# A five-layer graph network on one core: the second edge layer of the gathered group moved to the head of TensorE's step

## The reference

```python
def _leaky(x):
    return jax.nn.leaky_relu(x, negative_slope=0.1)
for l in range(W1.shape[0]):
    h = _leaky(x @ W1[l] + b1[l]) @ W2[l] + b2[l]
    e = _leaky(edge_attr @ We1[l] + be1[l]) @ We2[l] + be2[l]
    msg = h[src] * e * dot_scale[l]
    agg = jax.ops.segment_sum(msg, dst, num_segments=n)
    out = x + agg * res_w[l]
    mu = jnp.mean(out, axis=-1, keepdims=True)
    var = jnp.mean(jnp.square(out - mu), axis=-1, keepdims=True)
    x = (out - mu) * jax.lax.rsqrt(var + LN_EPS) * ln_g[l] + ln_b[l]
```

## Time and profile before

| | |
|---|---|
| median of 3 runs | 6457.28 us (6454.09 to 6462.97) |
| profiled execution | 6457.48 us, of which the trace's span is 6455.7 us |
| PE, matmuls | 5500.8 us busy, 85% of the span |
| DVE | 5171.0 us, 80% |
| POOL | 4527.6 us, 70% |
| ACT | 1134.5 us, 18% |
| mean granted clock of TensorE | 0.889 of 2.4 GHz |

### The profile page before, as it was taken

One profiled execution on the slowest core, in us unless ns is written; L12 is line 12 of the kernel. 1 busy time (PEld: TensorE's weight loads), 2 busy tenths in 40 slices (PEclk: granted clock), 3 DMA queues, 4 the chain that ended last, 5 costly groups with the idle time before them and its releaser, 6 DMA issues.

```text
span 6455.7 us, 169151 instructions
## 1 busy us (share of the span) xinstructions
PE 5500.8 (85%) x63332; PEld 3612.2 (56%) x63333; DVE 5171.0 (80%) x7991; ACT 1134.5 (18%) x1726; POOL 4527.6 (70%) x4793
## 2 busy tenths in 40 slices
PE   6776899998889788989878898888898887888887
PEld 2222444456666555666645666655566664556665
DVE  8997644598888688988859888867898885998886
ACT  0000311111222211122211122221112221111111
POOL 5777777766777367777737777756777773777775
PEclk9998555699999889999979999988999996999997
DMA  3112299855666455666635566644566663666664
GB/s 138 26 24 46 61 244 243 196 140 141 147 147 164 106 126 133 153 148 159 162 82 137 146 150 150 165 119 116 134 152 148 154 168 77 143 148 159 160 171 110
DMA packets 733545, 886.20 MB, mean 137 GB/s; under 512 B 325488, under 2 KB 502976, under 8 KB 731568
## 3 DMA queue, kind: packets, MB, share of 16 engines
q1 hardware_dynamic: 568480, 703.64, 42.4%
q0 software_dynamic: 152144, 154.93, 12.1%
q10 hardware_dynamic: 12096, 16.53, 0.8%
HBM read 749.51 MB, written 125.06 MB: 135 GB/s over the span
## 4 chain that ended last, share of the span: by engine, by line
PE 50%; DVE 18%; issue 14%; POOL 12%; DVEq 3%; ACT 2%; DMA 1%; ACTq 0%; SPq 0%; POOLq 0%
PE bank L981 12%; POOL arena L794 12%; PE bank L1030 8%; PE bank L1054 5%; PE bank L977 5%; PE bank L923 4%; PE bank L880 3%; PE bank L1017 3%; PE bank L861 2%; DVE arena L1765 2%; PE bank L846 2%; DVE arena L1423 2%; DVE arena L1677 2%; PE bank L902 2%; DVE arena L1432 2%
## 5 line engine op out<-in xcount | busy, mean ns | idle before, releaser
L794 POOL DMA_INDIRECT arena<-h_rows,src x3855 | 3674.2, 953 | 1555.7 <-issue 1246.5
L981 PEld LDWEIGHTS bank<-w2s,arena 128*128 128x128 f32 x8960 | 1143.7, 206 | 928.9 <-DVE arena L1765 694.9
L981 PE MATMUL bank<-w2s,arena 128*128 128x128 f32 x8960 | 1271.3, 298 | 412.5 <-DVE arena L1765 363.5
L781 POOL DMA_INDIRECT slots<-arena,slot_index x792 | 787.7, 995 | 267.2 <-issue 241.3
L1054 PEld LDWEIGHTS bank<-arena 112*64 112x64 f32 x20160 | 647.5, 139 | 287.9 <-issue 269.5
L1054 PE MATMUL bank<-arena 112*64 112x64 f32 x20160 | 733.2, 226 | 58.9 <-issue 53.8
L977 PE MATMUL bank<-x_packed,edge_w 64*128 64x512 f32 x1260 | 713.5, 647 | 0.8 <-DMA x_packed<-slot_attr 0.7
L1253 ACT ACTIVATE arena<-bank,tenth 128x512 f32<-128x512 f32 x490 | 335.6, 685 | 2125.1 <-PE bank L977 2125.1
L977 PE MATMUL bank<-nodes_state,edge_w 64*128 64x512 f32 x980 | 568.6, 661 | 105.5 <-DVE nodes_state L1746 66.6
L1685 DVE TENSOR_TENSOR x_packed<-bank,slot_rel 128x2880 f32<-128x2880 f32 (+8 forms) x315 | 592.4, 1881 | 49.3 <-issue 42.7
L1685 DVE TENSOR_TENSOR arena<-bank,slot_rel 128x2880 f32<-128x2880 f32 (+8 forms) x315 | 592.3, 1880 | 45.8 <-issue 39.3
(11 more groups left out here) (198 smaller groups left out, 5682.2 us busy)
## 6 DMA issues: line engine op xcount, KB each, us to landing
arena<-slot_pick SPq DMA_DIRECT2D x630, 448.0 KB
arena<-h_rows SPq DMA_DIRECT2D x630, 224.0 KB
x_packed<-slot_attr SPq DMA_DIRECT2D x630, 128.0 KB
nodes_state<-attr_t SPq DMA_DIRECT2D x485, 128.0 KB
arena<-h_rows,src POOLq DMA_INDIRECT x3855
slot_pick<-arena SPq DMA_DIRECT2D x126, 448.0 KB, 4.4
x_packed<-slots SPq DMA_DIRECT2D x127, 136.0 KB, 4.8
slots<-arena SPq DMA_DIRECT2D x9, 1904.0 KB, 22.1
```

Of the source, the lines that this page charges most:

```text
L781: pool.indirect_dma_start(slots, bass.IndirectOffsetOnAxis(ap=slot_index[:, t:t + 1], axis=0), records[:, v, j, :], None).then_inc(record_ ...
L794: pool.indirect_dma_start(to[0:n, at:at + D], None, table, bass.IndirectOffsetOnAxis(ap=index[0:n, t:t + 1], axis=0)).then_inc(landed(t), 16)
L981: mm = pe.matmul(to[:, j * P:(j + 1) * P], acts[:, j * TILE:(j + 1) * TILE], w2s[:, :], start=True, stop=True)
```

## The change

In PE's step the wait for the message and the second layer of the gathered group of step s+1 are moved ahead of the first layers of step s+2. Nothing else is moved, and the instructions are the same.

```diff
                 def step(s, part):
+                    now, m = a_at(s), a_at(s + 1)
+                    if now == SPILL_AT:
+                        pe.wait_ge(spill_msg_ready, l + 1)
+                    elif now is not None:
+                        pe.wait_ge(msg_ready, l * GR + real(now) + 1)
+                    if m is not None:
+                        pe.wait_ge(hid_acted[0], l * GA + m + 1)
+                        edge_out(hidden[:, 0, m % 2, :], e_ps).then_inc(e_ready, 1)
                     k = a_at(s + 2)
                     if k is not None:
                         pe.wait_ge(added, l * ADDS + adds_before(s) + 1)
...
                     if k is not None:
                         pe.wait_ge(slot_attr_landed[k % 2], 16 * (l * (NB // 2) + k // 2 + 1))
                         hidden_of(1, k, NB, slot_attr_in[:, k % 2, :])
-                    now, m = a_at(s), a_at(s + 1)
-                    if now == SPILL_AT:
-                        pe.wait_ge(spill_msg_ready, l + 1)
-                    elif now is not None:
-                        pe.wait_ge(msg_ready, l * GR + real(now) + 1)
-                    if m is not None:
-                        pe.wait_ge(hid_acted[0], l * GA + m + 1)
-                        edge_out(hidden[:, 0, m % 2, :], e_ps).then_inc(e_ready, 1)
                     k = b_at(s)
                     if k is not None:
                         pe.wait_ge(slot_msg_ready, l * NB + k + 1)
```

## The result

The changed kernel takes 7348.64 us (median of 4 runs, 7340.76 to 7354.55), the kernel before 6458.8 us (4 runs): a ratio of 1.138, 95% interval 1.137 to 1.140. That is 890 us more where 683 were forecast; the time lies in the range. The profiled execution has a span of 7352.7 us.

A forecast was written before the change was run, and what follows sets the result against it. No engine is full, the steps are a relay; DVE sets the pace where PE waits for its message. 6457.5 + 576 (351 + 70 + 155) + 107 for the clock = 7140 us, own range 6780 to 7465, with rivals 6760 to 7460.

The forecast's parts named there:

- the shadow of the message: Before the change, PE's first layers run while DVE is still at work, before PE can go on with DVE's message.
- steps in which PE waited for the message: 285 cases where PE stands ahead of the second layers until DVE's message; 1.23 us each, 351 us (228 to 427).
- the three kinds: Steps where PE waits: full, 1.7 us later; no gathered group in s+2, 1.3; none in s+1, 0.7.
- steps in which PE is late: 200 steps whose message is ready, or nearly, when PE arrives; 0.35 us each, 70 us (0 to 204).
- steps without a message: 155 steps without a gathered group of their own; second layer now precedes first, 1.0 us each, 155 us.
- the clock, 107 us: PE's longer gap before the message brings the low clock in one of ten of 485, 2.2 us each (0 to 213).
- the clock's rival: PE's clock falls most of the time; with four gaps in ten 427 us instead of 107, 7460 us; chance 0.17.
- the ring: Message, second layer, first layer, ACT, `acted`, rest of DVE's step, next message; in a full step `acted` comes 1.70 us later.
- the second way of counting: DVE waits 1.52 us in the mean at `acted`, gets back at most 0.64; 0.88 x 630 = 554 us.

The follow-up runs named there:

- wait_only: Kernel before, with only the wait for the gathered group's message moved ahead of the first layers, the second layer's four matmuls staying behind them; 7156.2 us, 1.110.
- slot_first: Changed kernel, but the slot group's first layer keeps its place ahead of the message wait, only the gathered group's going behind the second layer; 7287.2 us, 1.129.
- bias_first: Changed kernel, with DVE's bias of the gathered group put ahead of both `acted` instead of behind the slot group's bias; 7170.4 us, 1.111.
- the fillers: Changed kernel, with PE repeating the slot group's first layer ahead of the message wait, in whole (7236.3 us) or 256 of 512 columns (7280.4 us).
- before_swap: Kernel before, with DVE's bias of the gathered group put ahead of the slot group's bias; 6479.9 us, 1.0036.

## Why the prediction was right, and what it had too small

**Right: direction, place and mechanism.** The first layers leave the shadow of the message and enter a ring with ACT and DVE. DVE's wait for ACT's tenth and the timeline show it, and `wait_only` separates it: with all four matmuls in their old place the wait ahead of the first layers alone costs 702 us. The 0.00 us of the steps that `slot_first` leaves in their old order are the control. What comes earlier, the gathered group's second layer, was worth nothing in DVE's order, as said; only when DVE's order follows (`bias_first`) does it give 178 us.

**Right in size: steps in which PE waited for the message (term 351 us).** Counted by an idle time of PE ahead of L981, these are 298 steps in the timeline of before, and those of them that stayed at the high clock lost 1.18 us each, against 1.23. That the mean is so near is in part luck. By the 285 cases of the waits, with every single matmul counted, the three kinds lost 1.29, 1.18 and 1.03 us where 1.7, 1.3 and 0.7 were worked out: too much in full steps, too little where s+1 has no gathered group. And only 18 of the 92 full steps of this class stayed at the high clock.

**Too small: "steps in which PE is late", 0.35 us each.** Of the 177 others with a message, those at the high clock lost 0.90 us. The row I chose was a step without a second layer ahead of its first, where little moves; of the kinds that have one I said that DVE waits for PE anyway. It does not. PE's not waiting for the message does not mean that it came late. The timeline of DVE before, a full step of this class:

```profile
2573.67 0.68 DVE L1765 TENSOR_TENSOR arena<-arena,bank 128x512 f32<-128x512 f32 x1
...
2575.75 0.75 DVE L1677 SCALAR_TENSOR_TENSOR arena<-bank,edge_w,arena 128x512 f32<-128x512 f32 x1
...
2581.69 0.68 DVE L1765 TENSOR_TENSOR arena<-arena,bank 128x512 f32<-128x512 f32 x1
```

and PE's first layer in it:

```profile
2573.87 0.69 PE L977 MATMUL bank<-nodes_state,edge_w 64*128 64x512 f32 x1
```

The same step in the changed kernel, DVE:

```profile
2811.76 0.68 DVE L1765 TENSOR_TENSOR arena<-arena,bank 128x512 f32<-128x512 f32 x1
...
2815.53 0.75 DVE L1677 SCALAR_TENSOR_TENSOR arena<-bank,edge_w,arena 128x512 f32<-128x512 f32 x1 [1.76 <-ACT arena L1253]
...
2821.15 0.68 DVE L1765 TENSOR_TENSOR arena<-arena,bank 128x512 f32<-128x512 f32 x1
```

The first layer began 0.20 us after the message did, so nothing waited after it, yet it was just as much beside the message. `acted` goes from 2.08 to 3.77 us behind the message, the step from 8.02 to 9.39. With 0.90 in place of 0.35 the term is 159 us instead of 70.

**Too large: steps without a message**, 0.79 instead of 1.0 us, 118 instead of 155 us.

**Too small: the clock, 107 us.** I took one gap in ten. By first layers at the low clock it was 145 more of 625 steps, about three in ten of those with a message. The price was too high in turn: where the same step ran at both levels in different ones of the first four rounds (21 places), it was 1.25 us longer at the low one, and the fillers gave back 1.6 per case, against 2.2. So 145 x 1.25 to 1.6 = 181 to 232 us. The forecast's one in ten was too few, the four in ten of the clock's rival nearer, and the price of both too high; that rival's 7460 us was not reached.

The Trainium skill ("TensorE: Matmul & The Clock Gate", "A second HAM failure mode: psum-queue depth-cycling") tells of a kernel in which TensorE idled briefly between groups of matmuls so often that the clock swung between its two levels. The runs agree for gaps of this kind: behind gaps of 1.73 and 1.77 us the same step ran at either level, and the steps with a first layer at the low clock went from 9 to 154. What makes it one level or the other in a given round, no run shows.

Sum: 352 + 159 + 118 = 629, and 181 to 232 for the clock: 810 to 861 of 890. With every single matmul counted it is 610 us and 154 more cases at 1.6 us, 246: 856 of 893. The rest of 30 to 80 us stays open: the losses at the high clock are those of the steps that stayed there, and the others may have a larger loss from the ring.

**Wrong: the second way of counting.** It let DVE take back all its idle time at and behind `acted`, 0.64 us a step: 0.26 that was already at `acted` and 0.38 at L1681 and L1733. Of the 1091 us more at L1677 DVE got back 128 us from its waits for PE at L1681 and L1733, 0.20 us a step instead of 0.38, another 62 from "issue" at L1733, and a little elsewhere, so that 897 remained. A wait behind the delay shrinks only as far as its releaser is not delayed with it, and PE was: its window sums now wait 99.1 us for `acted`. The wait at `acted` was too small as well: 1.52 us a step were worked out, and it is 1263 / 630 = 2.0, with the clock in it. Both errors lower the figure, so it came out too low, and that its 554 us lay near the 576 of the sum confirmed nothing.

## What to carry to other kernels

Before moving work ahead of other work on an in-order engine, ask which of the two has the longer way back to that engine: here the first layer feeds ACT and DVE and belongs into the time in which PE would wait; what was put ahead of it feeds an instruction that nobody waits for yet. Judge whether work is in a wait's shadow by its start against the releaser's start, not by whether the engine idles after it. And count a longer gap on TensorE twice, once as a delay and once as a chance of the low clock behind it: here 1.6 us for each case. Before filling an engine's wait with other work, look at which wait stands next behind it: twice the filled wait came back there (`bias_first`, `before_swap`).

## What the runs showed of the hardware

- The same instructions behind the same gap (1.73 and 1.77 us) ran at the high clock in one round and at the low one in another. Of five rounds, the step shown was wholly at the high clock in one.
- The two first layers (64 rows of the array each, 512 columns) take 1.18 us side by side and 1.12 us each when the second layer stands between them (`slot_first`): the order of instructions decides whether PE does them in 1.18 or 2.24 us.
- Useless work in a gap of PE made the program faster in all five pairs of runs that differ by it alone: 112 and 68 us in the changed kernel, 41 with `bias_first`, 25 in the kernel before, 35 with `before_swap`.
